# Gates and bias product ahead of the up weights in a routed expert layer, and first block's output ahead of the second block's down product

## The chip, the cores and the metric

The kernel runs on one core of one Trainium2 chip. The metric is the device time of one execution in microseconds, here the median of three runs. Engines are named as in the profile: PE is TensorE (PEld its weight loads), DVE is VectorE, ACT is ScalarE, POOL is GpSimd, SP is SyncE.

## The reference

A sequence of 2048 rows of 128 goes through two layers, each an attention and a feed-forward part of experts, with a layer norm ahead of each part and the residual added behind it. The change touches the first layer's expert part, which picks two of eight experts for the whole sequence, by the mean of its normed rows:

```python
def _L0_ffn_ref(x, gate_w, down_w, down_b, up_w, up_b):
    pooled = x.mean(axis=1)
    gate = jax.nn.softmax(pooled @ gate_w.T, axis=-1)
    top_w, top_i = jax.lax.top_k(gate, TOP_K)
    top_w = top_w / (top_w.sum(axis=-1, keepdims=True) + 1e-08)
    Wd = down_w[top_i]; bd = down_b[top_i]
    Wu = up_w[top_i];   bu = up_b[top_i]
    h = jax.nn.gelu(jnp.einsum('bsd,bkcd->bksc', x, Wd) + bd[:, :, None, :], approximate=False)
    h = h * top_w[:, :, None, None]
    out = jnp.einsum('bksc,bkdc->bsd', h, Wu)
    out = out + (top_w[:, :, None] * bu).sum(axis=1)[:, None, :]
    return out

x = x + _L0_attn_ref(_layernorm(x, axis=-1), ...)
x = x + _L0_ffn_ref(_layernorm(x, axis=-1), ...)
x = x + _L1_attn_ref(_layernorm(x, axis=-1), ...)
x = x + _L1_ffn_ref(_layernorm(x, axis=-1), ...)
```

## The kernel before

The sequence is cut into 16 tiles of 128 rows, and these into 4 blocks of 512 (`NB` = 4, four tiles each). X, the residual, stays in SBUF for the whole kernel, as 128 partitions x 16 tiles x 128. The kernel is written by hand engine by engine: each engine has one list of instructions in a fixed order, and semaphores (`wait_ge`, `then_inc`) hold it to the others. PSUM is one tensor `ps` of eight banks. Nothing but this order and these waits decides what runs when.

The first attention takes the first 490 us or so. Then comes the expert part. In the order of TensorE's list (L1709 to L1816):

- The last rows of the normed input are summed, the logits are made (L1736), and VectorE finds the two largest, one small step at a time (L1200 to L1216). `g8[:, OH0:OH1+1]` are the two experts' one-hot rows, `g1[:, 5:7]` the two top weights, `g8[:, IDX]` in its last use the eight gates, of which six are zero.
- TensorE spreads the one-hot rows over partitions (L1775), VectorE makes four masks `sel` of them (L1207), and products with the masks pick the two experts: the down weights (L1783, to `sel_dT` by ScalarE at L699), their bias (L1786, to `sel_b` by VectorE at L1218), the gates over partitions (L1791, to `gb` by ScalarE at L702), the up weights (L1795, to `sel_uT` by ScalarE at L706, scaled by `top_w`), the two top weights over partitions (L1797, to `top_w` by VectorE at L1234), and the bias of the output (L1800, to `bias0` by ScalarE at L708). The helper `spin` makes products of `ident` with itself that nobody reads, into bank 6 or 7 (L1406); two of them stand ahead of L1783.
- For each block b, `hidden(b)` is the down product (L1751), ScalarE applies Gelu (L687) and `up(b)` is the up product (L1760). All four `up` write the same bank 4, so each waits for VectorE's add of the one before (`s_x2`). `hidden` has banks 6 and 7 in turn, and the Gelus two buffers.
- GpSimd adds `bias0` to each block of X (L962, signal `s_xb`), with its part of the next layer norm in between: add 0, add 1, norm steps of block 0, add 2, steps of 1, add 3, steps of 2 and 3. VectorE adds the expert's output (`stream0(b)`, L1229), takes the statistics of the block (`ln1_stats`, L300 and L307), and writes the norm of block 0 (`ln1_norm`, L333). ScalarE writes the norms of blocks 1 to 3 (L330), each when GpSimd has made its reciprocal deviation (L313, L315) and offset (L317, L320).
- TensorE transposes the norm by block (`ln1_T`, L339) and then starts on the second attention's scores (L1829), whose products for the first tile stand behind the transpose of block 1. In between it makes value weights for that attention (`value`, `values1`, L1713), which ScalarE copies (L680).

Of the kernel before, what the change touches and what calls it, by code (L numbers as in the profile page):

```python
# [6 lines left out]
ACT = mybir.ActivationFunctionType  # L7
# [5 lines left out]
P = 128  # L13
# [5 lines left out]
def build_kernel(nc, d, out):  # L19
# [13 lines left out]
    with ctx:  # L33
# [3 lines left out]
        def sem(name):  # L37
            return ctx.enter_context(nc.semaphore(name))
# [322 lines left out]
        s_h0_ps, s_h0, s_y0_ps, s_x2 = sem("s_h0_ps"), sem("s_h0"), sem("s_y0_ps"), sem("s_x2")  # L361
        s_half, s_yh, s_yT0 = sem("s_half"), sem("s_yh"), sem("s_yT0")
# [59 lines left out]
        with nc.Block() as block:  # L422
# [101 lines left out]
            def _(act):  # L524
# [175 lines left out]
                values1(0)  # L700
# [4 lines left out]
                act.wait_ge(s_tw, 1)  # L705
                act.activation(sel_uT[:, :], ps[:, 2, 0:D], ACT.Copy, scale=top_w[:, :]).then_inc(s_suT, 1)  # L706
                act.wait_ge(s_b0_ps, 1)
                act.copy(bias0[:, :], ps[:, 0, AT_BIAS:AT_BIAS + D]).then_inc(s_b0, 1)  # L708
                hidden(1)
# [291 lines left out]
            def _(dve):  # L1001
# [216 lines left out]
                dve.tensor_copy(sel_b[:, :], ps[:, 2, D:D + 1]).then_inc(s_selb, 1)  # L1218

# [5 lines left out]
                def stream0(b):  # L1225
# [4 lines left out]
                    ln1_stats(dve, b)  # L1230

                anchors_lo(0)
                dve.wait_ge(s_tw_ps, 2)
                dve.tensor_copy(top_w[:, :], ps[:, 2, AT_TW:AT_TW + 1]).then_inc(s_tw, 1)  # L1234
                anchors_lo(1)
                stream0(0)
                stream0(1)
                ln1_norm(dve, 0)
                stream0(2)
                ln1_lo(dve, 0, T1_BANK[0])  # L1240
                stream0(3)
                ln1_lo(dve, 1, T1_BANK[1])
# [148 lines left out]
            def _(pe):  # L1391
# [386 lines left out]
                spin(2, 6)  # L1778
# [5 lines left out]
                last.then_inc(s_sd_ps, 1)  # L1784
                for j in range(E // 2):
                    last = pe.matmul(ps[:, 2, D:D + 1], masks[j], down0_b[:, j:j + 1], start=(j == 0), stop=(j == E // 2 - 1))  # L1786
# [3 lines left out]
                pe.wait_ge(s_gv, 10)  # L1790
                pe.matmul(ps[0:E, 0, AT_GB:AT_GB + P], g8[:, IDX, :], ones_row[:, :], start=True, stop=True).then_inc(s_gb_ps, 1)  # L1791
                pe.wait_ge(s_selb, 1)
                pe.wait_ge(s_upx, 1)
                for j in range(E // 2):
                    last = pe.matmul(ps[:, 2, 0:D], masks[j], up_x[:, j, :], start=(j == 0), stop=(j == E // 2 - 1))  # L1795
                for k in range(2):
                    pe.matmul(ps[k * BN:(k + 1) * BN, 2, AT_TW:AT_TW + 1], ones_row[:, 0:BN], g1[:, 5 + k:6 + k], start=True, stop=True).then_inc(s_tw_ps, 1)  # L1797
                hidden(1)
                pe.wait_ge(s_gbc, 1)
# [225 lines left out]
```

## Time and profile before

| | |
|---|---|
| runs | 748.21, 748.12, 743.87 us; median 748.12 |
| profiled execution | 743.53 us, span of its instructions 741.8 us |
| PE busy | 718.9 us (97%) |
| DVE busy | 623.0 us (84%) |
| ACT busy | 471.8 us (64%) |
| POOL busy | 581.7 us (78%) |
| chain that ended last | PE 71%, POOL 13%, issue 9%, DVE 5%, ACT 1% |
| the expert part, from its masks to the first scores | about 504 to 521 us |

The times of a row count from the first instruction of the execution. A start of a PE row is where its first product is issued, and its duration runs to the end of the last, so that neighbouring PE rows overlap by the time a product takes to drain; in the chain's view these overlaps are taken off. A product of 32-bit numbers counts as two instructions, and the rows count both.

### The profile page before, as it was taken

To read this page: it belongs to the slowest core of one execution; us is meant where nothing else is said; L and a number is where in the kernel's file an instruction comes from. 1 tells how busy PE (TensorE), PEld (TensorE's weight loads), DVE (VectorE), ACT (ScalarE), POOL (GpSimd) and SP (SyncE) were. 2 spreads that over 40 slices of the span, in tenths; PEclk is the share of its full clock that TensorE was granted. 3 is DMA by queue.
4 is the path that set the end of the run, shared out by engine and by line. 5 is a ranking of instruction groups with operands and counts; after the bars stand their busy time and mean duration, and the time that the engine had idled before them with its cause. 6 is when DMAs were issued, how large, how long until landed. Compare 5 with 4: busy or idle time off the path is not lost.

```text
span 741.8 us, 12509 instructions
## 1 busy us (share of the span) xinstructions
PE 718.9 (97%) x4183; PEld 463.9 (63%) x4183; DVE 623.0 (84%) x1304; ACT 471.8 (64%) x1068; POOL 581.7 (78%) x484
## 2 busy tenths in 40 slices
PE   7999999999999999999999999999799999999997
PEld 6665555555555655555555555466566699778885
DVE  8888999999999999999999999765888636876785
ACT  4367767767767767677776776654677831455553
POOL 6488989989989989989999999953589851445664
PEclk9999999999999999999999999999999999999999
DMA  6200000000000000000000000012000000020330
GB/s 152 86 1 1 1 2 2 2 3 1 1 3 2 1 2 3 1 1 2 2 1 3 1 2 2 1 52 67 2 1 1 1 1 1 1 69 20 113 101 28
DMA packets 39575, 13.72 MB, mean 18 GB/s; under 512 B 27092, under 2 KB 36325, under 8 KB 39512
## 3 DMA queue, kind: packets, MB, share of 16 engines
q1 hardware_dynamic: 38232, 12.81, 7.3%
q8 instruction: 33, 0.54, 0.3%
q10 hardware_dynamic: 1280, 0.12, 0.1%
q14 instruction: 30, 0.25, 0.1%
HBM read 11.52 MB, written 1.08 MB: 17 GB/s over the span
## 4 chain that ended last, share of the span: by engine, by line
PE 71%; POOL 13%; issue 9%; DVE 5%; ACT 1%; POOLq 0%; DVEq 0%
PE ps L1472 18%; PE ps L1516 16%; PE ps L1458 15%; POOL hid_lo L997 7%; PE ps L1527 4%; PE ps L1867 4%; PE ps L1500 4%; POOL nrm L979 2%; POOL hid L979 1%; PE ps L1445 1%; PE ps L1446 1%; PE ps L339 1%; DVE mx L1051 1%; POOL up_x L973 1%; DVE mx L1045 1%
## 5 line engine op out<-in xcount | busy, mean ns | idle before, releaser
L1051 DVE TENSOR_REDUCE mx<-ps 128x1 f32<-128x512 f32 x492 | 307.6, 681 | 26.7 <-PE ps L1458 23.7
L618 ACT ACTIVATE prob<-ps 128x512 f32<-128x512 f32 x512 | 267.9, 606 | 76.7 <-PE ps L1472 76.7
L1472 PE MATMUL ps<-q_cols,key 128*128 128x512 f32 x512 | 213.7, 420 | 0.8 <-ACT prob L618 0.8
L1458 PE MATMUL ps<-key,q_rows 128*128 128x512 f32 x512 | 201.0, 397 | 0.8 <-DVE key L1037 0.5
L896 POOL TENSOR_TENSOR part<-part,prob 128x512 f32<-128x512 f32 x124 | 158.7, 1291 | 33.4 <-DVE part L1066 28.9
L1472 PEld LDWEIGHTS ps<-q_cols,key 128*128 128x128 f32 x512 | 95.6, 188 | 98.8 <-issue 49.9
L1516 PE MATMUL ps<-prob,val 128*32 128x512 f32 x1024 | 124.1, 598 | 0.0
L1458 PEld LDWEIGHTS ps<-key,q_rows 128*128 128x128 f32 x512 | 95.8, 188 | 20.1 <-DVE mx L1045 1.4
L896 POOL TENSOR_TENSOR part<-part,pair 128x512 f32<-128x512 f32 x64 | 95.6, 1494 | 0.1
L997 POOL TENSOR_TENSOR hid_lo<-hid,hid_hi 128x512 fp32r<-128x512 f32 x44 | 60.3, 1378 | 41.6 <-ACT hid_hi L780 41.5
L896 POOL TENSOR_TENSOR pair<-prob 128x512 f32<-128x512 f32 x64 | 82.4, 1288 | 1.9 <-ACT prob L618 1.9
L896 POOL TENSOR_TENSOR part<-prob 128x512 f32<-128x512 f32 x64 | 82.8, 1294 | 0.4 <-ACT prob L618 0.3
L1516 PEld LDWEIGHTS ps<-prob,val 128*32 128x32 f32 x1024 | 26.8, 109 | 60.9 <-issue 59.7
L764 ACT ACTIVATE act_g<-ps 128x512 f32<-128x512 f32 x44 | 26.4, 600 | 37.7 <-PE ps L1909 37.5
L1066 DVE TENSOR_TENSOR part<-prob 128x512 f32<-128x512 f32 x62 | 46.7, 754 | 0.3 <-ACT prob L618 0.3
L1357 DVE TENSOR_TENSOR prod<-ps,act_g 128x512 f32<-128x512 f32 x44 | 30.2, 686 | 17.1 <-PE ps L1909 14.6
L732 ACT ACTIVATE pT<-ps 128x128 f32<-128x128 f32 x128 | 33.7, 278 | 10.6 <-PE ps L1844 10.6
L596 ACT COPY u_sb<-ps 128x512 f32<-128x512 f32 x32 | 18.8, 589 | 33.9 <-PE ps L1516 33.9
L1100 DVE SCALAR_TENSOR_TENSOR X<-ps,rden,X 128x128 f32<-128x128 f32 x128 | 35.7, 342 | 1.0 <-PE ps L1500 0.7
L1907 PE MATMUL ps<-hT_hi,w_hi 128*128 128x512 f32 x88 | 35.5, 403 | 0.0
L1500 PEld LDWEIGHTS ps<-proj,u_sb 128*128 128x128 f32 x256 | 33.4, 191 | 2.5
L1909 PE MATMUL ps<-hT_lo,w_hi 128*128 128x512 f32 x88 | 34.6, 394 | 0.0
(285 smaller groups left out, 1144.1 us busy)
## 6 DMA issues: line engine op xcount, KB each, us to landing
den<-den_sb SPq DMA_DIRECT2D x124, 2.0 KB, 2.1
g_all<-g_rows SPq DMA_DIRECT2D x7, 256.0 KB, 3.3
X<-in_L_attn_h_t_dram SPq DMA_DIRECT2D x4, 256.0 KB, 4.1
out_dram<-X SPq DMA_DIRECT2D x4, 256.0 KB, 2.7
g_all<-g_rows SPq DMA_DIRECT2D x4, 224.0 KB, 3.1
w_raw<-in_L_ffn_w_g_dram SPq DMA_DIRECT2D x1, 704.0 KB, 4.5
w_raw<-in_L_ffn_w_u_dram SPq DMA_DIRECT2D x1, 704.0 KB, 6.2
w_raw<-in_L_ffn_w_d_dram SPq DMA_DIRECT2D x1, 704.0 KB, 8.1
```

What stands on the lines that cost most here:

```text
L618: act.activation(prob[:, g % RING, :], ps[:, g % 3, :], ACT.Exp, scale=SCALE).then_inc(s_exp, 1)
L896: pool.tensor_tensor(out, a, b, ALU.add).then_inc(s_sum, 1)
L997: pool.tensor_tensor(hid_lo[:, n % 4, :], hid[:, n % 2, :], hid_hi[:, n % 4, :].bitcast(F32), ALU.subtract).then_inc(s_hlo, 1)
L1051: dve.tensor_reduce(mx[:, n % 2, c % TPB, at:at + 1], ps[:, BANK["rows", 2 * lin + j], :], AX.X, ALU.max).then_inc(s_mrd, 1)
L1066: dve.tensor_tensor(part[:, n % 2, g, :], prob[:, t % RING, :], prob[:, (t + 1) % RING, :], ALU.add).then_inc(s_sumd, 1)
L1100: last = dve.scalar_tensor_tensor(out=xt, in0=ps[:, BANK["out", n], i * P:(i + 1) * P], scalar=rden[:, n % 2, i:i + 1], in1=xt, op0=ALU.mu ...
L1458: pe.matmul(ps[:, BANK["rows", 2 * lin + j], :], q_rows[:, k, i * P:(i + 1) * P], key[:, h % KBUF, c0:c0 + BLK], start=True, stop=True).th ...
L1472: pe.matmul(ps[:, g % 3, :], key[:, n // NB % KBUF, t * P:(t + 1) * P], q_cols[:, n % NB, :], start=True, stop=True).then_inc(s_sc, 1)
L1500: last = pe.matmul(ps[:, BANK["out", n], i * P:(i + 1) * P], u_sb[:, n % 2, i * P:(i + 1) * P], proj[:, n // NB, :], start=True, stop=True)
L1516: last = pe.matmul(ps[C * x:C * (x + 1), U, :], val[:, t, :], prob[:, (NT * n + t) % RING, :], start=(t < NG), stop=(t >= NT - NG))
L1907: pe.matmul(out_ps, w[0], x_hi, start=start, stop=False)
L1909: return pe.matmul(out_ps, w[0], x_lo, start=False, stop=stop)
```

## The change

On TensorE's list, the two filling products ahead of the down weights go. The products that spread the two top weights and the gates move ahead of the bias of the down product; the bias product of the output moves ahead of the up weights; and the up product of block 0 moves ahead of the down product of block 1. On VectorE's list, the copy of the top weights stands directly behind that of `sel_b`, and the norm of block 0 stands behind the add of block 1 but ahead of its statistics. On ScalarE's list, the copy of the output's bias moves ahead of the scaled up weights, and the first copy of value weights behind them. The new signal from the up weights to ScalarE uses a semaphore that has stood at 3 since the beginning. GpSimd's and SP's lists stay as they are.

```diff
@@ scalar
                 act.copy(sel_dT[:, :], ps[:, 3, 0:P]).then_inc(s_sdT, 1)
-                values1(0)
                 act.wait_ge(s_gb_ps, 1)
                 act.copy(gb[:, :], ps[0:E, 0, AT_GB:AT_GB + P]).then_inc(s_gbc, 1)
                 act.wait_ge(s_selb, 1)
                 hidden(0)
-                act.wait_ge(s_tw, 1)
-                act.activation(sel_uT[:, :], ps[:, 2, 0:D], ACT.Copy, scale=top_w[:, :]).then_inc(s_suT, 1)
                 act.wait_ge(s_b0_ps, 1)
                 act.copy(bias0[:, :], ps[:, 0, AT_BIAS:AT_BIAS + D]).then_inc(s_b0, 1)
+                act.wait_ge(s_tw, 1)
+                act.wait_ge(s_ux_ps, UX0 + 1)
+                act.activation(sel_uT[:, :], ps[:, 2, 0:D], ACT.Copy, scale=top_w[:, :]).then_inc(s_suT, 1)
+                values1(0)
                 hidden(1)
@@ vector
                 dve.tensor_copy(sel_b[:, :], ps[:, 2, D:D + 1]).then_inc(s_selb, 1)
+                dve.wait_ge(s_tw_ps, 2)
+                dve.tensor_copy(top_w[:, :], ps[:, 2, AT_TW:AT_TW + 1]).then_inc(s_tw, 1)
@@ vector
                     dve.tensor_tensor(xb, ps[:, 4, :].rearrange("p (i n) -> p i n", i=TPB), xb, ALU.add).then_inc(s_x2, 1)
-                    ln1_stats(dve, b)
 
                 anchors_lo(0)
-                dve.wait_ge(s_tw_ps, 2)
-                dve.tensor_copy(top_w[:, :], ps[:, 2, AT_TW:AT_TW + 1]).then_inc(s_tw, 1)
                 anchors_lo(1)
                 stream0(0)
+                ln1_stats(dve, 0)
                 stream0(1)
                 ln1_norm(dve, 0)
+                ln1_stats(dve, 1)
                 stream0(2)
+                ln1_stats(dve, 2)
                 ln1_lo(dve, 0, T1_BANK[0])
                 stream0(3)
+                ln1_stats(dve, 3)
                 ln1_lo(dve, 1, T1_BANK[1])
@@ tensor
-                spin(2, 6)
                 pe.wait_ge(ln0["hT"], NB + 3)
                 pe.wait_ge(s_pick, 1)
                 ...
                 last.then_inc(s_sd_ps, 1)
+                pe.wait_ge(s_gv, 8)
+                for k in range(2):
+                    pe.matmul(ps[k * BN:(k + 1) * BN, 2, AT_TW:AT_TW + 1], ones_row[:, 0:BN], g1[:, 5 + k:6 + k], start=True, stop=True).then_inc(s_tw_ps, 1)
+                pe.wait_ge(s_gv, 10)
+                pe.matmul(ps[0:E, 0, AT_GB:AT_GB + P], g8[:, IDX, :], ones_row[:, :], start=True, stop=True).then_inc(s_gb_ps, 1)
                 for j in range(E // 2):
                     last = pe.matmul(ps[:, 2, D:D + 1], masks[j], down0_b[:, j:j + 1], start=(j == 0), stop=(j == E // 2 - 1))
                 last.then_inc(s_su_ps, 1)
                 pe.wait_ge(s_sdT, 1)
                 hidden(0)
-                pe.wait_ge(s_gv, 10)
-                pe.matmul(ps[0:E, 0, AT_GB:AT_GB + P], g8[:, IDX, :], ones_row[:, :], start=True, stop=True).then_inc(s_gb_ps, 1)
+                pe.wait_ge(s_gbc, 1)
+                pe.matmul(ps[:, 0, AT_BIAS:AT_BIAS + D], gb[:, :], up0_b[:, :], start=True, stop=True).then_inc(s_b0_ps, 1)
                 pe.wait_ge(s_selb, 1)
+                pe.wait_ge(s_tw, 1)
                 pe.wait_ge(s_upx, 1)
                 for j in range(E // 2):
                     last = pe.matmul(ps[:, 2, 0:D], masks[j], up_x[:, j, :], start=(j == 0), stop=(j == E // 2 - 1))
-                for k in range(2):
-                    pe.matmul(ps[k * BN:(k + 1) * BN, 2, AT_TW:AT_TW + 1], ones_row[:, 0:BN], g1[:, 5 + k:6 + k], start=True, stop=True).then_inc(s_tw_ps, 1)
-                hidden(1)
-                pe.wait_ge(s_gbc, 1)
-                pe.matmul(ps[:, 0, AT_BIAS:AT_BIAS + D], gb[:, :], up0_b[:, :], start=True, stop=True).then_inc(s_b0_ps, 1)
+                last.then_inc(s_ux_ps, 1)
                 pe.wait_ge(s_suT, 1)
                 up(0)
+                hidden(1)
                 hidden(2)
```

TensorE's list from the filling products to the first up product, before. `sel` are the masks, `g` the small rows of gates, `hT` the normed input, `up_x` the up weights:

```order
L1406 MATMUL ps<-ident 128x128 x2
L1783 MATMUL ps<-sel,down 128x128 [waits s_pick,s_hT]
L1783 MATMUL ps<-sel,down 128x128 x3
L1786 MATMUL ps<-down_b,sel 128x1 x4
L1751 MATMUL ps<-hT,sel_dT 128x512 [waits s_acc,s_hT,s_sdT]
L1791 MATMUL ps<-ones_row,g 8x128 [waits s_gv]
L1795 MATMUL ps<-up_x,sel 128x128 [waits s_upx,s_selb]
L1795 MATMUL ps<-up_x,sel 128x128 x3
L1797 MATMUL ps<-g,ones_row 64x1 x2
L1751 MATMUL ps<-hT,sel_dT 128x512 [waits s_wa_lo,s_hT]
L1800 MATMUL ps<-up_b,gb 128x128 [waits s_gbc]
L1760 MATMUL ps<-sel_uT,hid 128x128 [waits s_hT,s_h0,s_suT]
```

And with the change, from the down weights on:

```order
L1788 MATMUL ps<-sel,down 128x128 x3
L1792 MATMUL ps<-g,ones_row 64x1 [waits s_gv]
L1792 MATMUL ps<-g,ones_row 64x1
L1794 MATMUL ps<-ones_row,g 8x128 [waits s_gv]
L1796 MATMUL ps<-down_b,sel 128x1 x4
L1757 MATMUL ps<-hT,sel_dT 128x512 [waits s_acc,s_hT,s_sdT]
L1801 MATMUL ps<-up_b,gb 128x128 [waits s_gbc]
L1806 MATMUL ps<-up_x,sel 128x128 [waits s_upx,s_tw,s_selb]
L1806 MATMUL ps<-up_x,sel 128x128 x3
L1766 MATMUL ps<-sel_uT,hid 128x128 [waits s_hT,s_h0,s_suT]
L1766 MATMUL ps<-sel_uT,hid 128x128 x3
L1757 MATMUL ps<-hT,sel_dT 128x512 [waits s_wa_lo,s_hT]
```

The gates (`8x128`) and top weights (`64x1`) have moved up ahead of `down_b`, the bias product (`up_b,gb`) ahead of the up weights, and one down product (`hT,sel_dT` with `s_wa_lo`) has moved from ahead of the up product to behind it. The filling products (`ident`) are gone.

VectorE's list from the last aggregate of block 0 to the norm of block 0, before. L1229 is the add of a block, BN_STATS and BN_AGGR are its statistics, L333 is the norm:

```order
L307 BN_AGGR mv<-stats 128x2 [waits s_ln1_st] x4
L1229 TENSOR_TENSOR X<-ps,X 128x512 [waits s_xb,s_y0_ps]
L300 BN_STATS stats<-X 128x6 [waits s_x2]
L300 BN_STATS stats<-X 128x6 x3
L307 BN_AGGR mv<-stats 128x2 [waits s_ln1_st] x4
L333 TENSOR_SCALAR hn<-X,mv,rstd 128x128 [waits s_ln1_rstd]
L333 TENSOR_SCALAR hn<-X,mv,rstd 128x128 x3
```

And with the change, where the add is L1234:

```order
L307 BN_AGGR mv<-stats 128x2 [waits s_ln1_st] x4
L1234 TENSOR_TENSOR X<-ps,X 128x512 [waits s_xb,s_y0_ps]
L333 TENSOR_SCALAR hn<-X,mv,rstd 128x128 [waits s_ln1_rstd]
L333 TENSOR_SCALAR hn<-X,mv,rstd 128x128 x3
L300 BN_STATS stats<-X 128x6 [waits s_x2]
L300 BN_STATS stats<-X 128x6 x3
L307 BN_AGGR mv<-stats 128x2 [waits s_ln1_st] x4
```

The four instructions of the norm stand directly behind the add of block 1; the statistics of block 1 follow them.

## Rows read from the trace of the kernel before

**Rows 1.** Stretches: length, then busy us (and instructions) by engine; clock, DMA

```profile
505.00:510.60 5.60, 5.60 (x37) 3.61 (x35) 1.90 (x7) 2.03 (x6) 0.00 (x0) 1.00 0.01 1
...
532.00:535.00 3.00, 0.35 (x3) 0.17 (x3) 2.96 (x4) 0.00 (x0) 2.77 (x2) 1.00 0.00 0
```

**Rows 2.** Chain that ended last, 503 to 522 us: start, duration, what

```profile
505.80 0.79 PE ps L1786 x8
506.59 0.97 PE ps L1751 x2
...
507.87 1.09 PE ps L1795 x8
508.95 0.21 PE ps L1797 x4
509.16 1.05 PE ps L1751 x2
510.22 0.43 PE ps L1800 x2
...
510.67 0.28 ACT bias L708
...
511.01 1.28 POOL X L962
...
512.38 0.70 DVE X L1229
...
514.38 0.70 DVE X L1229
...
519.66 1.08 PE ps L1713 x8
...
520.87 0.63 PE ps L339 x4
```

**Rows 3.** TensorE's timeline: start, duration, line, operation, [idle before and releaser]

```profile
504.75 1.06 PE L1783 MATMUL ps<-sel,down 128*128 128x128 f32 x8
...
507.49 0.38 PE L1791 MATMUL ps<-ones_row,g 1*8 1x128 f32 x2
...
510.56 1.16 PE L1760 MATMUL ps<-sel_uT,hid 128*128 128x128 f32 x8
```

**Rows 4.** VectorE's timeline: masks, sum of gates, aggregates and norm

```profile
503.70 0.69 DVE L1207 TENSOR_TENSOR sel<-half_eye,ps 128x512 f32<-128x512 f32 x1 [0.48 <-PE ps L1775]
...
505.48 0.15 DVE L1216 TENSOR_TENSOR g<-g 1x8 f32<-1x8 f32 x1
...
515.90 0.36 DVE L307 BATCH_NORM_AGGREGATE mv<-stats 128x2 f32<-128x6 f32 x4
516.17 1.61 DVE L333 TENSOR_SCALAR hn<-X,mv,rstd 128x128 f32<-128x128 f32 x4
```

**Rows 5.** GpSimd's timeline: norm steps of block 0, add 2, steps of block 1

```profile
514.34 0.23 POOL L313 TENSOR_SCALAR vare<-mv 128x4 f32<-128x4 f32 x1 [0.85 <-DVE mv L307]
...
515.66 1.27 POOL L962 TENSOR_TENSOR X<-X,bias 128x512 f32<-128x512 f32 x1
516.90 0.23 POOL L313 TENSOR_SCALAR vare<-mv 128x4 f32<-128x4 f32 x1
...
518.66 0.20 POOL L320 TENSOR_TENSOR nmr<-nmr,rstd 128x4 f32<-128x4 f32 x1
```

**Rows 6.** ScalarE's timeline: first Gelu, scaled up weights, norm of block 1

```profile
508.06 0.67 ACT L687 ACTIVATE hid<-ps,sel_b 128x512 f32<-128x512 f32 x1
509.43 0.37 ACT L706 ACTIVATE sel_uT<-ps,top_w 128x128 f32<-128x128 f32 x1 [0.69 <-DVE top_w L1234]
...
519.08 1.65 ACT L330 ACTIVATE hn<-X,nmr,rstd 128x128 f32<-128x128 f32 x4
```

**Rows 7.** VectorE: norm's first instruction alone; below, four of a norm elsewhere

```profile
516.17 0.84 DVE L333 TENSOR_SCALAR hn<-X,mv,rstd 128x128 f32<-128x128 f32 x1
...
498.96 1.11 DVE L333 TENSOR_SCALAR hn<-X,mv,rstd 128x128 f32<-128x128 f32 x4 [1.43 <-POOL rstd L315]
```

More of the change, by code:

```diff
@@ L361, in build_kernel @@
         s_h0_ps, s_h0, s_y0_ps, s_x2 = sem("s_h0_ps"), sem("s_h0"), sem("s_y0_ps"), sem("s_x2")
+        s_ux_ps, UX0 = s_zero, 3
         s_half, s_yh, s_yT0 = sem("s_half"), sem("s_yh"), sem("s_yT0")
```

## The prediction

> **What bounds the kernel now.** I began with the table of stretches, to see how large the changed part of the program is. It is the piece between the two attention layers, from about 504 to 521 us of a span of 741.8 us, 17 us or 2.3% of it. TensorE is busy for all of 5.60 us there and VectorE for 1.90, and the granted clock is 1.00, that is 2.4 GHz [rows 1]. But part of what keeps TensorE busy is work that nobody waits for yet, so its busy time is no limit. The chain of waits is what counts, and it was read next [rows 2]. It shows the order in which results released each other:
>
> - TensorE runs without a gap from the masks' down weights [rows 3] over the masks' down bias (505.80), the first block's down product, the gates, the up weights, the two top weights, the second block's down product and the bias product, whose last row begins at 510.22.
> - Then the bias is copied (510.67), GpSimd adds it to the first block of X (511.01), and only then VectorE adds the expert's output (512.38). That output was there before: TensorE made it from 510.56 for 1.16 us, thus by 511.72 [rows 3]. So the bias, and not the output, is what the first block waits for.
> - Behind it come the second block's output (514.38), the statistics of the second block, the norm of the first block (516.17 on VectorE) [rows 4], and at 520.87 the transpose of the second block of the norm, behind which all score products of the next layer stand on TensorE's queue.
>
> The last step is the one that passes any gain or loss on. That transpose needs the norm of block 1, which ScalarE writes from 519.08 for 1.65 us, to 520.73 [rows 6]. TensorE's own queue was done with the value products at 519.66 + 1.08 = 520.74 [rows 2]. Both arrive together, so a later norm costs at once, and a gain needs both to be earlier.
>
> **The change up to the first block.** I go through the new order, taking durations from the rows. A result passes from one engine to another in about 0.03 us to ScalarE (510.65 to 510.67), 0.07 to GpSimd (510.95 to 511.01) and 0.14 to TensorE (520.73 to 520.87) [rows 2, 6].
>
> - The filling products go. The down weights wait for the mask, which VectorE ends at 503.70 + 0.69 = 504.39 [rows 4]. They start at 504.53, where they started at 504.75 [rows 3]: 0.22 us earlier, result at 504.53 + 1.06 = 505.59.
> - The two top weights (0.21) follow, to 505.80. Then the gates. They wait for the sum of gates that VectorE ends at 505.48 + 0.15 = 505.63 [rows 4], so they begin at 505.77 and last 0.38 [rows 3], to 506.15. Down bias +0.79, to 506.94. First down product +0.97 to +1.05 by the two rows of it in the chain; with the larger, 507.99. It was 507.56 before, so it is 0.43 us later.
> - Bias product +0.43, to about 508.40. ScalarE is in the first Gelu from 508.02 for 0.67 us [rows 6] (before, 508.06), and copies the bias at 508.60 for 0.28. GpSimd starts its add at 508.94 instead of 511.01: 2.07 us earlier. First block with bias at 510.22.
> - Up weights +1.09, to 509.49. Scaling on ScalarE +0.03 + 0.37 [rows 6], to 509.89. First up product from 510.03 instead of 510.56 [rows 3], +1.16, to 511.19. VectorE adds it there at once, since the bias is in by 510.22. So block 0 of X is added at **511.19 instead of 512.38: 1.19 us earlier**. This is the gain at this point.
>
> **From there to the end of the piece.**
>
> - Second block. Its down product now stands behind the first up product: 511.19 + 0.97 = 512.16. Its Gelu takes 0.69, to 512.87, and the second up product runs from 513.01 for 1.16 us. VectorE adds it at 514.17 instead of 514.38. Of the 1.19 us, 0.21 are left on TensorE's way, because the down product, which was done ahead of time before, is now on the path.
> - Statistics of block 0: from the add to the last aggregate 1.52 + 0.36 = 1.88 us (514.38 to 515.90, and 0.36) [rows 4]. So 511.19 + 1.88 = 513.07, and GpSimd starts on it at 513.16 instead of 514.34. It begins the next bias add, of block 2, 1.32 us after that (514.34 to 515.66 before) [rows 5]: 514.48, until 515.75.
> - VectorE now does the norm of block 0 ahead of the statistics of block 1. It can begin at 514.17 + 0.69 = 514.86. But GpSimd's add has run since 514.48. What that does can be read from before: the norm's first instruction began at 516.17 inside such an add, took 0.84 us and ended just behind the add's end at 516.93 [rows 5, 7]. Four such instructions take 1.11 us together with no add beside them, and here the one took 0.84 [rows 7]. The whole norm ended 1.61 us after its start [rows 4], 0.85 behind the add's end. I take the same here: the norm ends at 515.75 + 0.85 = 516.60. This is a moved stall: 0.9 us of VectorE waiting for GpSimd, now ahead of the statistics of block 1 rather than behind them.
> - Statistics of block 1 from 516.50 (0.10 overlap, as 515.90 + 0.36 against 516.17), aggregates 0.79 later, +0.36: 517.65. Before, they were done at 516.26. GpSimd starts on them at 517.72 instead of 516.90 (there it was held by its own add until 516.93) [rows 5]. **This is 0.82 us later.** Its last step for block 1 began at 518.66, 1.76 behind, and took 0.20: now 519.48 to 519.68. ScalarE had 0.2 us of slack there (518.86 against 519.08). It writes the norm of block 1 from 519.72 for 1.65 us, to 521.37, and TensorE's transpose starts at **521.51 instead of 520.87: +0.64 us**.
> - Side branches. The bias add of block 3 stands behind the same GpSimd steps and ends at about 520.94, with VectorE's add of the last block behind it (0.8 us later). Its statistics end near 522.8, when the low part of block 1 comes due, so it stays just off the path. Block 0's own norm is earlier (516.60 against 517.78) and its transpose with it, but then TensorE waits for block 2's add (near 517.6 + 0.7) as it did. That gain ends in a wait of 0.9 us ahead of the transpose of block 1.
> - The value copy that moves behind the scaled up weights on ScalarE is 0.59 us long and is needed only when scores begin, after 521; it costs nothing unless it delays the second Gelu, and it ends at about 510.4 against 512.18. No DMA moves, and SP's and GpSimd's queues keep their order.
>
> The sum: +0.64 us on the profiled execution's 743.53, that is 744.17. On the median shown, 748.12, it is 748.76. The runs shown lie on two levels, 743.53 and 743.87, and 748.12 and 748.21, 4.5 us apart, so seven times the effect. I quote the median's, and the range must hold both levels.
>
> **The rivals.**
>
> - *The norm is not held.* Norm 514.86 to 515.97, statistics of block 1 done at 517.03, GpSimd at 517.12, norm of block 1 at 519.11, and the transpose at 520.9: +0.03, so 748.15 on the median. For it speaks that VectorE is at the norm within 0.4 us of the add's start, and that each of my starts may be off by 0.2. Against it, the row of 0.84.
> - *The gain arrives.* If the statistics of block 1 were not what the transpose waits for, the path would be TensorE's: with the norm behind the statistics as before, I get the statistics of block 1 done at 516.05, the third add at about 517.0, and the transpose at 520.15, so -0.7 us. The full 1.19 would need the second block to be as much earlier as the first. Time 747.4, at best 746.9. Against it is that the trace has the norm of block 1 and the value products within 0.01 us.
> - *TensorE's clock falls* (the one that ends clearly slower). The filling products keep TensorE busy; without them it idles for some 0.3 us at 504.3, 0.5 ahead of the first up product, 0.9 and 1.0 later. At half clock the 5.60 us of products in [rows 1] would take 11.2, and the 17 us of the piece up to twice as long, so the time would be 754 to 765. It decides only if such gaps are enough. From 532 to 535 TensorE is busy 0.35 of 3.00 us and its clock stays 1.00 [rows 1]. The Trainium skill, page "TensorE: Matmul & The Clock Gate", section "HAM oscillation — how this bites in real kernels", tells of kernels whose clock falls in waits between bursts; the rows show none here.
> - *Nothing.* That the change does nothing is not open: the order of the queues is different.
>
> **How the numbers follow.** My forecast +0.6 (0.3 to 1.0): 0.5. Norm not held, about 0: 0.2. Gain arrives, -0.7 to -1.2: 0.2. Clock: 0.02. The rest, 0.08, is some wait that I have not seen, of either sign. The predicted time is 748.8. The range takes the lower level with the full gain, 743.53 - 1.19 = 742.3, and the upper with +2, 750.2. A measurement of this kernel can tell about 1% from no change, 7.5 us; the lower level alone is 0.6% below the median. All cases but the clock stay within that, so faster 0.03, the same 0.94, slower 0.03.
>
> **What would show it.** In the profile of the changed kernel, with times counted from the first transpose of its stretch: GpSimd's first bias add 2.1 us earlier; the first output add 1.2 us earlier and bound by the up product, not by GpSimd; the first instruction of the norm of block 0 near 0.9 us long; the aggregates of block 1 1.4 us later; GpSimd's step on them 0.8 later; the transpose of block 1 waiting 1 us for ScalarE's norm. I am wrong if the norm's first instruction takes 0.3 us, if the transpose of block 1 is released by TensorE's own queue, or if the granted clock is below 1.00 anywhere between 504 and 525.

## The result, and the profile after

The changed kernel takes 747.60 us (median of 20 executions, 745.30 to 750.61), the kernel before, measured beside it, 744.19 us (20 executions, 743.48 to 748.43). The ratio is 1.0042, 95% interval 1.0030 to 1.0053: 3.1 us slower (3.4 by the medians). The time lies in the predicted range, 742.3 to 750.2, and within 1% of the predicted 748.8. That closeness is luck: the forecast stood on 748.12, the median of three executions, which is 3.9 us above that of twenty, and its +0.6 us was 2.8 short of the 3.4 by the medians. The two errors have opposite signs. The profile shows more: the case to which the prediction gave 0.02 is what happened.

The page of the changed kernel (span; busy share and count of each engine; granted clock in 40 slices):

```profile
span 747.7 us, 12502 instructions
...
PE 725.3 (97%) x4179; PEld 468.7 (63%) x4179; DVE 622.6 (83%) x1304; ACT 471.9 (63%) x1068; POOL 581.6 (78%) x484
...
PEclk9999999999999999999999999996999999999999
```

There is a 6 in the row of TensorE's clock, where before had only nines, and TensorE is busy for 6.4 us more with four instructions less. The table of stretches finds the place (columns as in [rows 1]):

```profile
502.00:504.00 2.00, 1.88 (x16) 1.53 (x17) 1.09 (x8) 1.26 (x3) 0.00 (x0) 1.00 1.19 305
504.00:505.00 1.00, 0.73 (x7) 0.57 (x6) 0.90 (x5) 0.99 (x3) 0.00 (x0) 1.00 0.74 177
505.00:506.00 1.00, 1.00 (x8) 1.00 (x6) 0.51 (x3) 0.20 (x2) 0.00 (x0) 0.52 0.00 0
506.00:512.00 6.00, 6.00 (x22) 3.61 (x22) 1.42 (x4) 1.45 (x4) 0.00 (x0) 0.50 0.02 4
512.00:518.00 6.00, 5.48 (x19) 4.16 (x19) 1.70 (x9) 0.87 (x3) 2.49 (x2) 0.50 0.00 0
518.00:519.00 1.00, 1.00 (x2) 0.26 (x2) 0.14 (x3) 0.66 (x1) 0.68 (x2) 0.66 0.00 0
519.00:521.00 2.00, 2.00 (x12) 1.17 (x10) 0.84 (x2) 0.69 (x1) 1.82 (x2) 1.00 0.00 0
```

From 505 on the clock is 0.50, the 1.2 GHz level, until past 518, and TensorE is busy for every bit of it but the wait for the scaled up weights. Added up in slices of 1 us, the clock was low for 13.6 us. The prediction had named just this as a sign of being wrong, a granted clock below 1.00 anywhere between 504 and 525. Just ahead of the fall TensorE was busy 0.73 of 1 us, from 504 to 505. In this stretch of before it was busy throughout:

```profile
504.00:505.00 1.00, 1.00 (x10) 0.88 (x9) 0.90 (x5) 0.99 (x4) 0.00 (x0) 1.00 0.71 171
```

The chain of waits of the changed kernel, from the masks on:

```profile
503.83 0.70 DVE sel L1210
504.53 0.14 issue
504.66 1.71 PE ps L1788 x8
...
507.20 1.80 PE ps L1796 x8
509.00 1.92 PE ps L1757 x2
...
511.63 2.02 PE ps L1806 x8
...
514.16 2.08 PE ps L1766 x8
516.23 3.00 PE ps L1757 x4
519.23 0.90 PE ps L1766 x8
...
520.85 1.02 DVE hn L333 x4
...
523.02 0.24 POOL vare L313
...
525.02 1.66 ACT hn L330 x4
...
526.81 0.63 PE ps L339 x4
```

This answers [rows 2, 3]. The down weights start 0.83 us after the masks (503.83 to 504.66), 0.22 earlier than before, as forecast; but they last 1.71 us instead of 1.06. The down bias takes 1.80 for 0.79, the up weights 2.02 for 1.09, the first up product 2.08 for 1.16. The transpose of block 1 starts at 526.81, which is 22.98 us behind the start of the masks' instruction; before, it was 17.17 (503.70 to 520.87). So the piece is 5.81 us longer, and the profiled execution, 749.46 us against 743.53, is 5.93 longer. From that transpose to the last instruction both take 220.9 us.

VectorE's and GpSimd's timelines answer [rows 4, 5, 7]. The first block is now added when the up product ends, and not when the bias does:

```profile
516.27 0.69 DVE L1234 TENSOR_TENSOR X<-ps,X 128x512 f32<-128x512 f32 x1 [5.75 <-PE ps L1766]
...
520.16 0.69 DVE L1234 TENSOR_TENSOR X<-ps,X 128x512 f32<-128x512 f32 x1 [2.02 <-PE ps L1766]
520.77 1.11 DVE L333 TENSOR_SCALAR hn<-X,mv,rstd 128x128 f32<-128x128 f32 x4
```

```profile
512.01 2.49 POOL L965 TENSOR_TENSOR X<-X,bias 128x512 f32<-128x512 f32 x2 [12.53 <-ACT bias L707]
...
519.55 1.27 POOL L965 TENSOR_TENSOR X<-X,bias 128x512 f32<-128x512 f32 x1
```

The norm of four took 1.11 us, with no stall. GpSimd's add of block 2 began at 519.55 and ended at 520.82, as VectorE reached the norm at 520.77: with products at half speed the second block came so late that the add was over. So this profile says nothing on the stall that the sum rested on; that had to be made visible by experiment.

### The profile page after: what moved, and what is told of

The parts are those of the page before. It is cut to its first block, busy times and chain, and to the rows that moved or that the text cites. A ratio compares the mean times of both kernels' runs of the same rounds, so it can differ in the third digit from the quotient of the medians.

```text
span 747.7 us, 12502 instructions
## 1 busy us (share of the span) xinstructions
PE 725.3 (97%) x4179; PEld 468.7 (63%) x4179; DVE 622.6 (83%) x1304; ACT 471.9 (63%) x1068; POOL 581.6 (78%) x484
## 3 DMA queue, kind: packets, MB, share of 16 engines
HBM read 11.52 MB, written 1.08 MB: 17 GB/s over the span
## 4 chain that ended last, share of the span: by engine, by line
PE 71%; POOL 13%; issue 9%; DVE 5%; ACT 1%; DMA 0%; POOLq 0%; ACTq 0%
PE ps L1478 18%; PE ps L1522 16%; PE ps L1464 15%; POOL hid_lo L1000 7%; PE ps L1533 4%; PE ps L1875 4%; PE ps L1506 4%; POOL nrm L982 2%; POOL hid L982 1%; PE ps L1451 1%; PE ps L1452 1%; POOL sel L976 1%; DVE mx L1054 1%; PE ps L1757 1%; POOL up_x L976 1%
```

## The experiments

All were measured beside the kernel before, 99 more executions of it (median 744.40, 743.37 to 748.75). Each execution has a mean granted clock. Of those 99, 37 have 0.998 or more; of these, 32 take 743.4 to 743.9 us (743.6 in the middle), which is called the time at full clock. The other five take 745.2 to 745.3, for a reason that no profile shows. 11 lie above 746, all at 748.3 to 748.8 with a clock of 0.989 to 0.991. The last column counts the executions above 746 us. Such a count, and a mean clock, don't say where in the execution the clock was low; only the profiled execution of each run does, and no execution of before above 746 was profiled.

| kernel | filling ahead of down weights | order | median (n) | at full clock | above 746 |
|---|---|---|---|---|---|
| before | 2 | old | 744.40 (99) | 743.6 | 11 of 99 |
| changed, both measurements | 0 | new | 747.37 (28) | none | 23 of 28 |
| e1 | 0 | old | 746.57 (12) | 743.55 | 7 of 12 |
| e2 and e12 | 2 | new | 745.61 (20) | 744.4 to 744.6 | 6 of 20 |
| e3 | 2 | new, norm old | 743.91 (12) | 743.1 to 743.25 | 1 of 12 |
| e4 | 2 | e3, down product old | 744.02 (12) | none, lowest 743.38 | 1 of 12 |
| e5 | 2, but 3.4 us earlier | new | 748.36 (6) | none | 5 of 6 |
| e6 | 4 | old | 745.12 (11) | 744.2 to 744.4 | 2 of 11 |
| e7 | 0 | new, norm old | 747.26 (12) | 742.8 to 743.0 | 8 of 12 |
| e8 | 2, and 3 more in later gaps | new, norm old | 744.00 (12) | 743.03 | 1 of 12 |
| e9 | 2 | new, add 2 early | 743.83 (12) | 743.6 to 743.7 (4 of 5) | 0 of 12 |
| e10 | 2 | e4, add 2 early | 743.35 (12) | 742.2 to 742.5 | 1 of 12 |

### Is it the filling products?

e1 takes only them from the kernel before:

```diff
                 value(0, 3).then_inc(s_wv_ps, 1)
-                spin(2, 6)
                 pe.wait_ge(ln0["hT"], NB + 3)
```

> The kernel before, without the two filling products ahead of the down weights; every order as before. In the profile of the changed kernel the granted clock is 0.50 from about 505 to 518 us. Theory A, the missing filling products let the clock fall: the clock falls here too, near 505, for 6 to 20 us, and the time is 1.5 to 6 us above the kernel before. Theory B, the new order of the products is what lets it fall (the small products, of one column, stand closer together): the clock stays 1.00, and the time is 0.0 to 0.3 us below the kernel before.

746.57 us, ratio 1.0019 (1.0001 to 1.0037). One execution at full clock, 743.55; seven of twelve at 746.5 to 748.0 with clocks of 0.991 and 0.992. The rise, 2.2 us by the medians and 1.4 us by the means (746.09 against 744.66), is at the lower end of what theory A said, 1.5 to 6. Theory B's 0.0 to 0.3 us below holds only for the one execution at full clock. The profiled execution, 744.45 us, was one of the five that are not long:

```profile
504.00:505.00 1.00, 0.73 (x7) 0.57 (x6) 0.90 (x5) 0.99 (x4) 0.00 (x0) 1.00 0.74 179
505.00:519.00 14.00, 12.80 (x79) 8.80 (x79) 8.43 (x34) 6.75 (x15) 6.84 (x10) 1.00 0.01 2
531.00:539.00 8.00, 5.99 (x19) 3.52 (x17) 7.61 (x11) 3.23 (x15) 6.03 (x5) 0.57 0.00 0
```

Here TensorE idled by 0.27 us at 504.4 as in the changed kernel, and the clock stayed 1.00; it was low only from 531 to 539, in the scores' stage, and once more at the very end. So without the filling products the clock need not fall near 505. That they make long executions likelier, the counts show, 7 of 12 against 11 of 99; where the clock of e1's seven was low, no profile shows.

e2 puts them back into the changed kernel at their old place:

```diff
                 value(0, 3).then_inc(s_wv_ps, 1)
+                spin(2, 6)
                 pe.wait_ge(ln0["hT"], NB + 3)
```

> The changed kernel with the two filling products put back at their old place. Theory A: the clock stays 1.00, and what is left is the cost of the order, which the prediction's chain puts at +0.6 us less 0.0 to 0.2 over the kernel before (743.5 to 744.8 there), with the first instruction of the norm of block 0 held to near 0.9 us. Theory B: the clock falls as in the changed kernel, and the time is 2 to 5 us above. A rival within A: the extrapolation of the changed kernel's 20 runs to a clock of 1.00 ends at about 743.1, so the order alone may be faster than before by 0.5 to 1 us.

745.76 us, ratio 1.0014 (0.9999 to 1.0030). Executions at full clock are back, at 744.38, 744.45 and 744.62, 0.9 us above before's 743.6. At full clock theory A holds, and the order costs 0.8 to 1.0 us there, somewhat more than the 0.4 to 0.6 of the chain; the rival from extrapolating the changed kernel's times to full clock (743.1) does not hold. But five of the twelve are above 746, so A's clock of 1.00 does not hold for all.

e5 puts them back too, but at another place, joined to the eight that stand ahead of the pooling product:

```diff
-                spin(8, 6)
+                spin(10, 6)
                 pe.wait_ge(ln0["hn"], 2 * NT)
```

> The changed kernel with the two filling products put back, but 3.4 us earlier, behind the eight that stand ahead of the pooling products; at the old place, ahead of the down weights, TensorE still idles for 0.27 us. Theory A1, it is the idle piece just ahead of the down weights that lets the clock fall: the clock falls as in the changed kernel, near 505, in nearly every execution, and the time is 745.3 to 750.6. Theory A2, it is how busy TensorE was over a longer piece: the two products do their work here too, and the time is that of the kernel with the filling products back at their place (744.4 at full clock, median 745.8). They also delay the pooling product by up to 0.55 us if TensorE is what it waits for.

748.36 us, ratio 1.0049 (1.0033 to 1.0064), six executions, none below 745.8:

```profile
504.00:505.00 1.00, 0.73 (x5) 0.57 (x6) 0.89 (x3) 0.99 (x3) 0.00 (x0) 1.00 0.59 139
505.00:519.00 14.00, 13.48 (x46) 9.19 (x46) 3.95 (x17) 3.38 (x9) 2.82 (x4) 0.51 0.01 1
```

Again 13.7 us of low clock, from 505.1 on. The same two products 3.4 us earlier keep nothing in these six executions, so what counts is that they stand close ahead of the down weights: A1, not A2.

e6 asks for the dose, with four in the kernel before:

```diff
-                spin(2, 6)
+                spin(4, 6)
                 pe.wait_ge(ln0["hT"], NB + 3)
```

> The kernel before with four filling products instead of two. The down weights start 0.55 us later, so at full clock the time is 743.6 + 0.5 = 744.1. The kernel before shows executions of 748.4 us with a mean clock of 0.989 to 0.991 in 4 of 35; without the filling products 7 of 12 are at 0.991 or 0.992. If filling products are what keeps the clock here, none of the executions is near 748.5, and the median is 744.1 to 744.8. If the two were enough or don't matter, the share near 748.9 stays about 1 in 9.

745.12 us, ratio 1.0015 (1.0006 to 1.0024). At full clock 744.24 and 744.40, 0.7 us above before. Of these, the profile accounts for 0.45: the down weights start 1.49 us behind the masks for 1.05, and the transpose of block 1 17.62 for 17.17. None of eleven is near 748.5, where before has one in nine; with eleven executions this may be chance. Two lie at 746.62. More filling than two costs more than it brings.

e7 takes only the norm's place back from the changed kernel, so that the filling products stay out:

```diff
                 stream0(1)
-                ln1_norm(dve, 0)
                 ln1_stats(dve, 1)
+                ln1_norm(dve, 0)
```

> The changed kernel, still without filling products, but with the statistics of block 1 ahead of the norm of block 0 again. By the runs so far, the place of the norm costs 1.3 us at full clock (744.45 against 743.2). If the clock falls near 505 because of the missing filling products and the order of the small products, it falls here too (0.987 to 0.996), and the time is 744 to 749.5, about 1 us under the changed kernel. If the norm's place and the waits behind it are what lets the clock fall, executions at 1.00 come back, near 743.

747.26 us, ratio 1.0027 (1.0005 to 1.0049). Twelve executions in two groups: four at 742.76 to 743.77, eight at 746.3 to 748.9. The profile, of 747.30 us:

```profile
504.00:506.00 2.00, 1.73 (x17) 1.42 (x16) 1.38 (x7) 1.36 (x5) 0.00 (x0) 1.00 0.41 100
506.00:517.00 11.00, 10.48 (x33) 6.91 (x32) 3.26 (x13) 2.49 (x7) 2.63 (x3) 0.53 0.00 1
```

So without the filling products the clock falls near 505 under this order as well, in the profiled execution; by their times, 746.3 to 748.9, seven more of the twelve are like it. And the two at full clock are faster than before by 0.6 to 0.8 us. e3, below, is this kernel with the filling products. Against it, they cost about 0.3 us at full clock (two executions each) and turn 8 of 12 long executions into 1 of 12.

e11 looks at the changed kernel again:

> The changed kernel once more, for the place at which its clock falls in other executions. In the first profile it was 0.50 from 505 to 518.6. If that fall is what costs, an execution of 749 to 750.6 has 13 us or more at 0.50 there, one of 747 about 7 to 10 us, and one of 745.3 to 745.5 none there, but one behind 530 (0.996).

Eight executions, 745.39 to 748.12, median 746.64. The profiled one took 747.86:

```profile
506.00:517.00 11.00, 10.48 (x33) 7.01 (x32) 3.26 (x13) 2.39 (x7) 2.58 (x3) 0.53 0.00 1
517.00:519.00 2.00, 2.00 (x12) 1.19 (x10) 0.42 (x1) 1.01 (x2) 1.92 (x3) 1.00 0.00 0
```

The low stretch is 10.2 us long here, from 506.4 on, where the one of 749.46 had 13.6. This is what was expected for the first, and roughly for the second; an execution near 745.4 was not caught in a profile. Against the 744.2 that the order alone should give without filling products (e2's 744.45 less the 0.3), the two cost 3.7 and 5.3 us: 0.36 to 0.39 us for each microsecond at 0.50. But in both the stall of the norm is all but gone (1.11 and 1.15 us for 2.02), which hides some 0.9 us of the cost. e7 has no stall at either clock: 747.30 against its 742.9 at full clock, thus 0.43 us for each of its 10.2. With all of the stretch bound by products it would be 0.5.

### What the order costs

e2's profile, which has the clock at 1.00 up to 537, shows the stall that the sum rested on. VectorE's add of block 0 and norm, GpSimd's add of block 2, and TensorE's transpose of block 1:

```profile
511.78 0.69 DVE L1234 TENSOR_TENSOR X<-ps,X 128x512 f32<-128x512 f32 x1 [2.66 <-PE ps L1766]
...
515.19 2.02 DVE L333 TENSOR_SCALAR hn<-X,mv,rstd 128x128 f32<-128x128 f32 x4
```

```profile
515.19 1.24 DVE L333 TENSOR_SCALAR hn<-X,mv,rstd 128x128 f32<-128x128 f32 x1
```

```profile
515.08 1.27 POOL L965 TENSOR_TENSOR X<-X,bias 128x512 f32<-128x512 f32 x1
```

```profile
522.14 0.63 PE L339 MATMUL ps<-ident,hn 128*128 128x128 f32 x4 [0.94 <-ACT hn L330]
```

The norm took 2.02 us, its first instruction alone 1.24. It began 0.11 behind GpSimd's add, and ended at 517.21, 0.86 behind the add's end at 516.35; the prediction said 0.85. The transpose stands 18.14 us behind the masks (504.00), 0.97 more than before's 17.17, and was released by ScalarE's norm of block 1 after a wait of 0.94. Its clock, for the record:

```profile
505.00:519.00 14.00, 12.51 (x79) 8.78 (x78) 8.29 (x32) 7.13 (x15) 5.57 (x7) 1.00 0.01 2
537.00:541.00 4.00, 4.00 (x11) 2.44 (x10) 3.41 (x6) 3.71 (x18) 3.33 (x3) 0.57 0.00 0
```

e3 has the norm behind the statistics again, on top of e2 (the diff of e7):

> The changed kernel with the two filling products, and with the statistics of block 1 ahead of the norm of block 0 again on VectorE. If the place of the norm costs what the prediction says, this is 1.3 us faster than the one that only has the filling products back (the transpose of block 1 0.7 us earlier than in the kernel before, instead of 0.6 later). If GpSimd doesn't hold the norm up, it is 0.7 us faster than that. If the place doesn't matter, the two are equal within 0.2 us.

743.91 us, ratio 0.9988 (0.9968 to 1.0007), and 743.09 and 743.25 at 0.998. Against e2 at full clock it is 1.3 us faster, the number of the first reading. The norm is not held, and the transpose stands at 16.60 us behind the masks (503.94), 0.57 less than before:

```profile
516.32 1.08 DVE L333 TENSOR_SCALAR hn<-X,mv,rstd 128x128 f32<-128x128 f32 x4
```

```profile
520.54 0.66 PE L339 MATMUL ps<-ident,hn 128*128 128x128 f32 x4
```

e4 also puts the down product of block 1 back ahead of the up product of block 0:

```diff
+                hidden(1)
                 pe.wait_ge(s_suT, 1)
                 up(0)
-                hidden(1)
                 hidden(2)
```

> As the one before (filling products, old place of the norm), and with the down product of block 1 ahead of the up product of block 0 again, so that of the change only the earlier top weights, gates and bias product are left. The down product stands in a time in which TensorE would wait for the scaled up weights (0.5 us), so block 0 is added 0.4 us later than in that one, but block 1 0.6 us earlier. If the second block is what the path goes by, this is 0.3 to 0.7 us faster than that one and the fastest of the four; if the first block is, it is 0.4 us slower.

744.02 us, ratio 0.9996 (0.9979 to 1.0013); no execution at full clock. By its profile block 1 is added 9.86 us behind the masks (503.89 to 513.75), in e3 10.58 (503.94 to 514.52), as expected; but the norm runs into GpSimd's add (515.03 to 516.30) and takes 1.61 us, where e3's took 1.08. Of the 0.7 us, 0.26 are left at the transpose (520.23, that is 16.34 behind the masks), and the times don't show them (its profiled execution has a low stretch from 534 to 538, and what that costs stands below):

```profile
513.75 0.69 DVE L1234 TENSOR_TENSOR X<-ps,X 128x512 f32<-128x512 f32 x1
...
515.54 1.61 DVE L333 TENSOR_SCALAR hn<-X,mv,rstd 128x128 f32<-128x128 f32 x4
```

e9 tests the stall by moving the other side. GpSimd adds blocks 0, 1 and 2 in a row, and block 3 behind the steps of blocks 0 and 1; the rest is e2:

```diff
                 for b in range(NB):
+                    if b == NB - 1:
+                        ln1_pool(pool, 0)
+                        ln1_pool(pool, 1)
                     xb = X[:, TPB * b:TPB * (b + 1), :]
                     pool.tensor_tensor(xb, xb, bias0[:, :].unsqueeze(1).to_broadcast([P, TPB, D]), ALU.add).then_inc(s_xb, 1)
-                    if b >= 1:
-                        ln1_pool(pool, b - 1)
+                ln1_pool(pool, NB - 2)
                 ln1_pool(pool, NB - 1)
```

> The changed kernel with the two filling products back, and with GpSimd's bias add of block 2 ahead of its norm steps of block 0 and the add of block 3 behind those of block 1. In the kernel without this the norm of block 0 took 2.02 us beside an add, against 1.08 with none beside it. Theory H, the add holds the norm: here no add runs beside it, it takes 1.1 us, the transpose of block 1 starts 0.9 us earlier, and the lowest time is 743.5 against 744.4. Rival, the norm is slow for another reason (the first use of its operands, say): it stays at 2.0 us, and the lowest time stays at 744.4.

```profile
514.96 1.11 DVE L333 TENSOR_SCALAR hn<-X,mv,rstd 128x128 f32<-128x128 f32 x4
```

```profile
509.35 3.71 POOL L968 TENSOR_TENSOR X<-X,bias 128x512 f32<-128x512 f32 x3 [9.92 <-ACT bias L707]
...
519.12 1.27 POOL L968 TENSOR_TENSOR X<-X,bias 128x512 f32<-128x512 f32 x1
```

```profile
520.99 0.63 PE L339 MATMUL ps<-ident,hn 128*128 128x128 f32 x4 [0.56 <-ACT hn L330]
```

The norm takes 1.11 us for 2.02, the transpose stands 17.22 us behind the masks (503.77) instead of 18.14, and the lowest time is 743.56 for 744.38. Theory H holds to 0.1 us: GpSimd's add holds VectorE's norm up, and that was the cost of the order. The edit moves other GpSimd steps too, but the rival, a norm that is slow for a reason of its own, is excluded by the 1.11. The median is 743.83, ratio 0.9986 (0.9970 to 1.0001). No execution of twelve is above 746, where e2 and e12 have six of twenty; that may be chance, and no profile shows those six.

e10 joins this to e4 (both diffs):

> The kernel with the filling products, the old place of the norm and the down product of block 1 ahead of the up product of block 0 (lowest 743.38, norm of block 0 1.61 us beside an add), with the same order on GpSimd as the one before this. Theory H: the norm takes 1.1 us and the transpose of block 1 starts 0.5 us earlier; lowest time 742.8 to 743.0, and median 743.3 to 743.7, which would be the fastest kernel of this study, 0.7 us under the kernel before. Rival: no change, 743.4 lowest.

```profile
519.52 0.66 PE L339 MATMUL ps<-ident,hn 128*128 128x128 f32 x4
```

The norm takes 1.08 us for e4's 1.61, as theory H has it. The transpose is at 15.88 us behind the masks (503.64), 1.29 less than before, and the times at full clock are 742.17, 742.29 and 742.54: 1.1 to 1.4 us under before's 743.6. The median is 743.35, ratio 0.9988 (0.9970 to 1.0006), lower than forecast at full clock and as forecast in the median, because nine of the twelve have a mean clock below 0.998, so a low stretch somewhere. It is the fastest kernel of the study at full clock; against before the interval reaches 1.

### Two that settled little

e8 adds to e3 three filling products where TensorE idles: one ahead of the logits' product and two ahead of the first up product.

```diff
                 last.then_inc(s_pool_ps, 1)
+                spin(1, 6)
...
+                spin(2, 3)
                 pe.wait_ge(s_suT, 1)
                 up(0)
```

> The kernel with the two filling products and the old place of the norm (743.91 us median, 743.09 lowest), with three more filling products where TensorE idles: one ahead of the logits' product and two ahead of the first up product, where it waits 0.52 us for the scaled up weights. If idling in this piece is what leaves the slow executions (745.8 and 748.6 of twelve), they go, and the median is 743.1 to 743.9, under the kernel before by 0.5 to 1 us. If these products delay the path, the lowest time rises by 0.1 to 0.4. If the clock falls elsewhere, nothing changes.

744.00 us, ratio 1.0000 (0.9985 to 1.0016), 743.03 at full clock, one of twelve at 749.05. They cost nothing and brought nothing that twelve executions can tell.

e12 is e2 once more:

> The changed kernel with the two filling products back, once more. Its times of 747.0 to 747.3 (clock 0.994, 3 of 12) have not been seen in a profile. If they are a fall near 505 cut short, the filling products only make it rarer; if they lie at 518 to 525, it is the waits ahead of the transposes (1 us each), which the place of the norm made, that let the clock fall there. If the profile falls on a time below 746, the only low stretches are behind 530.

Its profiled execution, 745.39 us, had its low stretches only behind 530 (6.8 us between 532 and 540, and the end). The times from 746.4 to 747.3 of e2 were not caught, so where their clock is low is open.

### What a low stretch behind 530 costs

The fourteen profiles together give the price of a low stretch behind 530. From the transpose of block 1 to the last instruction, the nine with the clock at 1.00 from 531 to 541 take 220.8 to 221.0 us. The five with a low stretch there (e1, e2, e4, e6, e12) take 221.9 to 222.0, so 1 us more, be the stretch 3.4 or 6.8 us long. None of the four whose clock fell near 505 has one there too. 41 of the 99 executions of before, with mean clocks of 0.993 to 0.997, lie at 744.1 to 744.9, about 1 us above the time at full clock. This stretch would explain them, but none of them was profiled.

## Why the prediction was right, and where it was not

- **The class and the range** were right; the range because it took in both levels of before's runs. The likeliest size was not: +0.6 forecast, +3.1 measured. That the predicted time is only 1.2 us off is luck, as said above: a base too high and an effect too small.
- **First block 1.19 us earlier.** Right. In e2, whose filling products put back 0.2 of it, the add of block 0 is 7.78 us behind the masks, against 8.68 before (503.70 to 512.38) and 7.49 forecast.
- **0.21 us left at the second block.** Right: 10.58 behind the masks in e2 against 10.68 before, forecast 10.47; the difference is again the filling.
- **The norm held by GpSimd's add, 0.85 us behind its end.** Right at full clock, to 0.01 us (e2), and shown by moving the add (e9). The norm met the add sooner than forecast, 0.11 us behind its start and not 0.38, so its first instruction took 1.24 us and not near 0.9. Here the rule cited from the Trainium skill, page "SBUF — State Buffer", section "SBUF: two separate sides", agrees with the trace. In the changed kernel's own profiled execution the two met for only 0.05 us, since the low clock had shifted them apart.
- **Transpose of block 1 +0.64.** e2 has +0.97, of which the filling products that the forecast left out are up to 0.22; at full clock the order costs 0.9 us.
- **"The gain arrives", -0.7.** This was worked out with the norm behind the statistics, and e3 has just that: -0.57 in the trace.
- **The step that failed is the rival of the clock**: its chance, 0.02, and the reason for it. The prediction said that "from 532 to 535 TensorE is busy 0.35 of 3.00 us and its clock stays 1.00". That was one execution. In the profiled executions of e1, e2, e4, e6 and e12, whose order in that stage is before's, the clock is low in that stage, for 3.4 or 6.8 us, and costs 1 us. The kernel before itself has a lower mean clock in most of its executions. The 748.1 and 748.2 us that stood beside 743.5 and 743.9 from the beginning were the sign: the prediction took the two levels as something to hold in the range, and not as a question, and it called the difference larger than the effect. The executions of before at 748.3 and more all have clocks of 0.989 to 0.991. The change moved the share above 746 from 1 in 9 to 4 in 5, and in all profiles of it (two) and of its variants without filling at that place (e5, e7) the clock was low from 505 or 506 on.
- **The price of the fall** was mis-sized the other way: 754 to 765 forecast, on half the clock for the whole piece. The low stretch is 10 to 14 us long and not all of it is bound by products. It costs 3.7 to 5.3 us against the changed order at full clock, and 0.9 more that the vanished stall hides.
- **Why the filling products matter.** That they do is shown, for their place and presence (e1, e2, e5, e7); by what rule the clock falls in one execution and not in the next is not. Whether the changed kernel falls more often than e1 and e7 is open. It has 23 of 28 above 746 against their 15 of 24, but its order costs 0.9 us in itself, and above 747 it is 16 of 28 against 12 of 24.

The sum of it, by the means of all executions: changed 747.56 (28) less before 744.66 (99) is 2.9 us. The order with the filling products kept is 745.71 over the 20 executions of e2 and e12, +1.05. The other 1.85 us are the filling products' absence.

## What to carry to other kernels

Ahead of taking out work that nobody reads, look at the spread of the times and not at one trace: two levels of times, with the mean clock of each execution beside them, say whether the clock is lost in some executions, which one profile with nines throughout can't say. When VectorE's work on SBUF is moved forward, look at what GpSimd does at that moment: a norm of 1.1 us became one of 2.0 beside an add, and moving the add cured it. And judge a reorder at the place where two chains meet; the first block came 1.2 us earlier, and the transpose that counts 0.6 to 1.0 later.

## What the runs showed of the hardware

- With TensorE idle for 0.27 us ahead of the down weights, in a stretch of small products, the clock fell to the 1.2 GHz level in four of five profiles (changed, e5, e7, e11; not e1). It fell 0.2 to 0.4 us after the down weights started in two of them and 1.6 to 1.8 us after in the other two, though TensorE was busy without a break in between. With two products that nobody reads in that gap it stayed at 1.00 there in all eight profiles that have them, and executions above 746 us are rare (1 of 12 in e3, against 8 of 12 in e7). The same products 3.4 us earlier don't help (e5).
- Once fallen, the clock stayed low for 10.2 or 13.6 us of nearly unbroken products before it rose.
- Where it falls differs between executions of one kernel: in the changed kernel at 505.0 in one profile and at 506.4 in the other, in e2 and e12, which are one kernel, for 3.4 us from 537 on or for 6.8 us from 532 on. The Trainium skill, page "TensorE: Matmul & The Clock Gate", section "What's actually happening", says that the chip's watching of TensorE runs free of the kernel's start, so that the same kernel can meet it at another point each time. The spread of these runs agrees.
- A low clock costs what TensorE's products lose that others wait for: 4.4 us for 10.2 us near 505 (e7), 1 us for either 3.4 or 6.8 us between 531 and 541 (five profiles), and nothing at the end of the program, where in e3, of 743.25 us, it is low for the last 3.1 us and TensorE has no product left.
- GpSimd's add of 128x512 on SBUF holds up VectorE's norm that starts inside it: four instructions took 2.02 us (e2), 1.61 (before, e4) and 1.15 (e11) by how early they met it, and 1.08 to 1.11 with no add beside them (e3, e9, e10). Where it was held, the norm ended 0.84 to 0.86 us behind the add's end. VectorE's own add, with one input in PSUM, was not held: 0.70 us beside GpSimd's add in before (512.38), and as much in e2 with only its last 0.2 beside one.
